# Halving the first sequence's opening: transposes, split and decay products by half the rows

## The reference

```python
h = rmsnorm(xn, pre_norm_w)
a = sigmoid(h @ w_a + decay_bias)           # decay
i = sigmoid(h @ w_i); v = h @ w_v
s = sqrt(clip(1 - a*a, 1e-8)) * (i * v)
rec = chunked_scan(a, s)                    # state = a * state + s
y = xn + rec @ out_proj_w
attn = y + (silu(gate) * up) @ w_down       # gate, up = rmsnorm(y) @ w_gate_up
moe = top-2 of 8 experts, each relu(xn @ w_fc)**2 @ w_proj, router logits xn @ w_router
```

## Time and profile before

| what | value |
|---|---|
| median of 3 runs | 288.89 us (288.81 to 288.93) |
| span of the profiled execution | 286.9 us |
| median less span | 1.99 us |
| PE busy | 279.4 us, 97% of the span |
| DVE, ACT, POOL busy | 202.7, 170.9, 145.8 us |
| granted PE clock | 9 tenths or more in all 40 slices |

### The profile page before, as it was taken

The page is one execution under the profiler, slowest core; times in us unless marked ns, Lnnn a source line. Parts: engine busy times, 40 slices in busy tenths (PEclk is TensorE's granted clock), DMA queues, the critical chain, the costliest instruction groups (busy, mean ns, idle before and its releaser), DMA issues.

```text
span 286.9 us, 5651 instructions
## 1 busy us (share of the span) xinstructions
PE 279.4 (97%) x1825; PEld 249.2 (87%) x1825; DVE 202.7 (71%) x467; ACT 170.9 (60%) x365; POOL 145.8 (51%) x138
## 2 busy tenths in 40 slices
PE   6999999999999999999999899999999999999995
PEld 5888988888988898898998789989989999888895
DVE  3899899989988978836558686555446545446973
ACT  3797967999759555536675545437477545432331
POOL 5498020433750135864877777666786776620000
PEclk9999999999999999999999999999999999999999
DMA  6999990017995011444244444344344534449922
GB/s 210 344 377 383 386 409 0 0 11 113 243 267 115 0 40 39 76 68 64 56 77 70 75 64 73 62 69 61 61 78 77 84 62 56 55 84 358 331 75 73
DMA packets 32584, 36.92 MB, mean 129 GB/s; under 512 B 4390, under 2 KB 29740, under 8 KB 32524
## 3 DMA queue, kind: packets, MB, share of 16 engines
q0 software_dynamic: 9616, 13.01, 28.2%
q1 hardware_dynamic: 20672, 21.31, 22.4%
q10 hardware_dynamic: 2268, 2.23, 2.2%
HBM read 24.68 MB, written 13.96 MB: 135 GB/s over the span
## 4 chain that ended last, share of the span: by engine, by line
PE 90%; DVE 5%; POOL 2%; issue 2%; ACT 1%; POOLq 0%; ACTq 0%; DVEq 0%
PE ps L396 75%; PE ps L656 6%; PE ps L479 5%; PE ps L400 1%; PE ps L492 1%; PE ps L413 1%; DVE hT_lo L1087 1%; POOL rn L1504 1%; DVE Wpj_lo L1247 1%; DVE stats L1059 0%; DVE X L1080 0%; DVE dec L1118 0%; POOL Waiv_raw L1541 0%; PE ps L507 0%; DVE xgT_lo L1322 0%
## 5 line engine op out<-in xcount | busy, mean ns | idle before, releaser
L1552 POOL DMA_INDIRECT xg<-xh_dram,gather_u x39 | 46.6, 1195 | 47.4 <-DVE picks L1314 34.8
L1561 POOL DMA_INDIRECT acc_dram<-yb,gather_u x39 | 61.9, 1587 | 16.3 <-issue 9.4
L396 PE MATMUL ps<-h2T_lo,Wgu_hi 128*128 128x512 f32 (+1 forms) x132 | 42.9, 386 | 0.0
L396 PE MATMUL ps<-h2T_hi,Wgu_hi 128*128 128x512 f32 (+1 forms) x132 | 40.9, 391 | 0.0
L396 PE MATMUL ps<-h2T_hi,Wgu_lo 128*128 128x512 f32 (+1 forms) x132 | 40.1, 385 | 0.0
L396 PE MATMUL ps<-Wd_hi,guT_hi 128*128 128x256 f32 x128 | 36.3, 284 | 0.1
L1331 DVE TENSOR_TENSOR aT_lo<-ps,aT_hi 128x256 fp32r<-128x256 f32 x39 | 16.6, 425 | 27.9 <-ACT aT_hi L911 21.1
L396 PE MATMUL ps<-Wd_hi,guT_lo 128*128 128x256 f32 x128 | 36.1, 282 | 0.0
L396 PE MATMUL ps<-Wd_lo,guT_hi 128*128 128x256 f32 x128 | 36.1, 282 | 0.0
L1252 DVE TENSOR_TENSOR gu<-gu,ps 128x512 f32<-128x512 f32 x31 | 21.2, 684 | 14.0 <-PE ps L396 10.9
L869 ACT ACTIVATE gu<-ps 128x512 f32<-128x512 f32 x31 | 18.4, 595 | 20.2 <-PE ps L396 20.2
(11 more groups left out here) (190 smaller groups left out, 683.7 us busy)
## 6 DMA issues: line engine op xcount, KB each, us to landing
sums<-acc_dram SPq DMA_DIRECT2D x8, 512.0 KB, 7.8
acc_dram<-zero SPq DMA_DIRECT2D x1, 2176.0 KB, 14.8
Wgu_raw<-in_L_attn_w_gate_up_dram SPq DMA_DIRECT2D x4, 512.0 KB, 9.3
Wfc_raw<-in_L_ffn_w_fc_dram SPq DMA_DIRECT2D x4, 512.0 KB, 13.7
xh_dram<-X ACTq DMA_DIRECT2D x4, 512.0 KB, 7.9
Wpj_raw<-in_L_ffn_w_proj_dram SPq DMA_DIRECT2D x4, 512.0 KB, 9.8
X<-in_L_attn_x_dram SPq DMA_DIRECT2D x3, 512.0 KB, 6.3
out_dram<-X SPq DMA_DIRECT2D x3, 512.0 KB, 4.8
```

What stands on the lines that cost most here:

```text
L396: return nc.tensor.matmul(dst, lhs, rhs, start=start, stop=stop, skip_group_check=group)
L1552: pool.indirect_dma_start(out=xg[i % XG][:, :], out_offset=None, in_=xh_dram, in_offset=bass.IndirectOffsetOnAxis(ap=gather_u[:, i:i + 1], ...
L1561: pool.indirect_dma_start(out=acc_dram[i % 2], in_=yb[i % YB][:, :], in_offset=None, compute_op=ALU.add, out_offset=bass.IndirectOffsetOnA ...
```

## The change

In the first sequence (b = 0) three steps go by halves `h` of its rows (row tiles 0 and 1, then 2 and 3), each half 256 rows wide. `transpose_first(h)` transposes a half into a pair of banks of its own (0 and 1, then 4 and 5). `split_first(h)` makes the high part of both feature blocks of that half in one ACT instruction, and the low part in one DVE instruction. `first_gates(h, part)` does the products of n = 0 and n = 1 for that half: part 0 those with the high activation (8 matmuls 256 wide), part 1 those with the low one (4 matmuls). DVE normalises row tiles 1, 2 and 3, ACT only tile 0. The 6 fillers stand behind the first half's transposes, the 12 in front of the products are gone. Semaphore counts are shifted to match.

```diff
--- before.py
+++ after.py
@@ -216,6 +216,7 @@
         var_ready, rstd_ready = sem("var_ready"), sem("rstd_ready")
         xh_ready, xh_half = [sem(f"xh_ready{b}") for b in range(B)], sem("xh_half")
         xh_stored = [sem(f"xh_stored{b}") for b in range(B)]
+        xT_half, hT_first_hi, hT_first_lo = sem("xT_half"), sem("hT_first_hi"), sem("hT_first_lo")
         xT_done, hT_hi, hT_split, wr_hi, wr_split = sem("xT_done"), sem("hT_hi"), sem("hT_split"), sem("wr_hi"), sem("wr_split")
         logit_done, logit_copied = sem("logit_done"), sem("logit_copied")
         tables_ready, q_ready = sem("tables_ready"), sem("q_ready")
@@ -400,24 +401,47 @@
                     nc.tensor.matmul(ps[:, bank, 0:P], ones_bf[:, :], before[:, :], start=True, stop=True)
 
             def transpose_x(c):
-                if c:
-                    pe.wait_ge(xh_ready[c], 1)
-                    pe.wait_ge(hT_split, K * c)
-
-                for j in (0, 1, 3, 2) if c == 0 else range(J):
-                    if (c, j) == (0, 3):
-                        keep_clock(6, 7)
-                    if c == 0:
-                        pe.wait_ge((xh_ready[0], xh_half)[j % 2], j // 2 + 1)
+                pe.wait_ge(xh_ready[c], 1)
+                if c > 1:
+                    pe.wait_ge(hT_split, K * (c - 1))
+
+                for j in range(J):
                     for k in range(K):
                         last = nc.tensor.transpose(ps[:, TX + k, j * P:(j + 1) * P], X[c][:, j, k * P:(k + 1) * P],
                                                    ident[:, :])
                 last.then_inc(xT_done, 1)
 
+            def transpose_first(h):
+
+                for j in (2 * h, 2 * h + 1):
+                    pe.wait_ge(*((xh_ready[0], 1) if j == 0 else (xh_half, j)))
+                    for k in range(K):
+                        last = nc.tensor.transpose(ps[:, TX + 4 * h + k, (j % 2) * P:(j % 2 + 1) * P],
+                                                   X[0][:, j, k * P:(k + 1) * P], ident[:, :])
+                last.then_inc(xT_half, 1)
+
+            def first_gates(h, part):
+
+                cols = slice(h * S // 2, (h + 1) * S // 2)
+                if part == 0:
+                    pe.wait_ge(hT_first_hi, h + 1)
+                else:
+                    pe.wait_ge(hT_first_lo, h + 1)
+                for l in (0, 1) if part == 0 else (0,):
+                    for k in range(K):
+                        if h == 0 and part == 0:
+                            pe.wait_ge(w_first_lo if l else w_half, k + 1)
+                        for n in range(2):
+                            last = product(ps[:, rec_bank(0, n), cols], Waiv[l][:, k, n * P:(n + 1) * P],
+                                           hT[0][part][:, k, cols], h + part + l + k == 0, part == 1 and k == K - 1, True)
+                            if h == part == 1 and k == K - 1:
+                                last.then_inc(aiv_done, 1)
+
             def logits(c):
 
-                pe.wait_ge(hT_split, K * (c + 1))
-                if c == 0:
+                if c:
+                    pe.wait_ge(hT_split, K * c)
+                else:
                     pe.wait_ge(wr_split, 1)
                 for j in range(J):
                     t = J * c + j
@@ -432,31 +456,19 @@
             def aiv(b, n):
 
                 what, r = n // 2, n % 2
-                if n == 0 and b:
-                    pe.wait_ge(hT_hi, K * (b + 1))
+                if n == 0:
+                    pe.wait_ge(hT_hi, K * b)
                 p = 6 * b + n - 5
                 if p >= 0:
                     pe.wait_ge(*rec_taken(p // 6, p % 6))
                 col = what * D + r * P
-                if (b, n) == (0, 0):
-
-                    pe.wait_ge(w_hi, 1)
-                    for k in range(K):
-                        pe.wait_ge(hT_hi, k + 1)
-                        for l in range(2):
-                            if l == 1:
-                                pe.wait_ge(w_first_lo, k + 1)
-                            product(ps[:, rec_bank(0, 0), :], Waiv[l][:, k, 0:P], hT[0][0][:, k, :], k + l == 0, False)
-                    for k in range(K):
-                        pe.wait_ge(hT_split, k + 1)
-                        last = product(ps[:, rec_bank(0, 0), :], Waiv[0][:, k, 0:P], hT[0][1][:, k, :], False, k == K - 1)
-                for m, (l, h) in enumerate((PRODUCTS if b == 0 else ((0, 0), (1, 0), (0, 1))) if b + n else ()):
+                for m, (l, h) in enumerate(PRODUCTS if b == 0 else ((0, 0), (1, 0), (0, 1))):
                     if b == 0 and m == 0 and r == 0:
-                        pe.wait_ge(w_hi, what + 1)
+                        pe.wait_ge(w_hi, what)
                     if b == 0 and l == 1 and r == 0:
                         pe.wait_ge(w_lo, what)
                     if n == 0 and m == 2:
-                        pe.wait_ge(hT_split, K * (b + 1))
+                        pe.wait_ge(hT_split, K * b)
                     for k in range(K):
                         last = product(ps[:, rec_bank(b, n), :], Waiv[l][:, k, col:col + P], hT[b][h][:, k, :],
                                        m + k == 0, m == 2 and k == K - 1)
@@ -468,7 +480,7 @@
                     pe.wait_ge(rec_ready, K * (b + 1))
                     if b == 0:
                         pe.wait_ge(wo_loaded, 16)
-                        pe.wait_ge(hT_split, K * B)
+                        pe.wait_ge(hT_split, K * (B - 1))
                     elif b == 1:
                         pe.wait_ge(routed, 1)
                         pe.wait_ge(count_taken, 1)
@@ -591,10 +603,13 @@
             pe.wait_ge(smalls_loaded, 48)
             nc.tensor.transpose(ps[:, 6, 0:3 * K], small_rows[:, :], ident[0:3 * K, 0:3 * K]).then_inc(smalls_turned, 1)
             keep_clock(8, 7)
-            transpose_x(0)
-            keep_clock(12, 7)
-            aiv(0, 0)
-            aiv(0, 1)
+            transpose_first(0)
+            keep_clock(6, 7)
+            first_gates(0, 0)
+            transpose_first(1)
+            first_gates(0, 1)
+            first_gates(1, 0)
+            first_gates(1, 1)
             aiv(0, 2)
             aiv(0, 3)
             logits(0)
@@ -763,7 +778,7 @@
                     act.wait_ge(w_loaded[0], 16)
                 hi, lo, raw = pieces[0][1]
                 A.activation(hi[:, k, :], raw[:, k, :], ACT.Copy,
-                             scale=smalls[:, PRE_W + k:PRE_W + k + 1]).then_inc(*((w_half, 1) if k == 0 else (w_hi, 1)))
+                             scale=smalls[:, PRE_W + k:PRE_W + k + 1]).then_inc(w_half, 1)
 
             def weights_hi(n):
                 if n == UNDER_SCAN:
@@ -787,6 +802,12 @@
                 A.activation(X[0][:, 2 * h, :], X[0][:, 2 * h, :], ACT.Identity, scale=rn1[:, 2 * h:2 * h + 1],
                              bias=nb1[:, 2 * h:2 * h + 1]).then_inc(xh_ready[0], 1)
 
+            def split_first(h):
+                act.wait_ge(xT_half, h + 1)
+                cols = slice(h * S // 2, (h + 1) * S // 2)
+                A.activation(hT[0][0][:, :, cols], ps[:, TX + 4 * h:TX + 4 * h + 2, 0:S // 2],
+                             ACT.Copy).then_inc(hT_first_hi, 1)
+
             def normalise_x(c):
                 act.wait_ge(rstd_ready, c + 2)
                 for j in range(J):
@@ -796,13 +817,13 @@
                 last.then_inc(xh_ready[c], 1)
 
             def store_xh(c):
-                act.wait_ge(xh_ready[c], 1 if c else 2)
+                act.wait_ge(xh_ready[c], 1)
                 if c == 0:
-                    act.wait_ge(xh_half, 2)
+                    act.wait_ge(xh_half, 3)
                 act.dma_start(xh_t[c], X[c][:, :, :]).then_inc(xh_stored[c], 16)
 
             def split_h(c):
-                act.wait_ge(xT_done, c + 1)
+                act.wait_ge(xT_done, c)
                 if c == 3:
                     act.wait_ge(aiv_done, 6)
                 for k in range(K):
@@ -926,9 +947,9 @@
             normalise_first(0)
             act.wait_ge(smalls_ready, 1)
             gates_hi_first(0)
-            normalise_first(1)
             gates_hi_first(1)
-            split_h(0)
+            split_first(0)
+            split_first(1)
             weights_hi(1)
             weights_hi(2)
             split_router()
@@ -1069,9 +1090,15 @@
             def normalise_first(h):
 
                 dve.wait_ge(rstd_ready, h + 1)
-                t = 2 * h + 1
-                V.tensor_scalar(X[0][:, t, :], X[0][:, t, :], mv[:, t, 0:1], rn1[:, t:t + 1],
-                                ALU.subtract, ALU.mult).then_inc(xh_half, 1)
+                for t in (1,) if h == 0 else (2, 3):
+                    V.tensor_scalar(X[0][:, t, :], X[0][:, t, :], mv[:, t, 0:1], rn1[:, t:t + 1],
+                                    ALU.subtract, ALU.mult).then_inc(xh_half, 1)
+
+            def split_first(h):
+                dve.wait_ge(hT_first_hi, h + 1)
+                cols = slice(h * S // 2, (h + 1) * S // 2)
```

(10 more changed lines are left out.)

## The result

| | before | after |
|---|---|---|
| median of 7 runs | 288.81 us (288.14 to 289.01) | 289.63 us (289.41 to 290.94) |
| ratio | | 1.0039, 95% interval 1.0025 to 1.0052 |
| span of the profiled execution | 286.9 us | 287.8 us |
| start of `transpose_x(2)` in the trace | 20.77 | 21.60 |

The change makes the kernel slower: by 0.82 us (0.3%) by the medians, by 1.1 us (0.39%, interval 0.7 to 1.5 us) by the ratio. The forecast was 289.8 in 289.3 to 290.3, slower with a chance of 0.75. In the traces `transpose_x(2)` starts 0.83 later and the span is 0.9 longer, so the loss is made before that point, and nothing behind it gives it back.

A forecast was written before the change was run, and what follows sets the result against it. The prediction took PE to bound the kernel (busy 97% of the span), with POOL's path meeting PE's at `transpose_x(2)`. POOL's root, 0.90 us late, carried through: 288.89 + 0.90 = 289.8 us, range 289.3 to 290.3.

The forecast's parts named there:

- The place in PE's queue: Second half's transposes queue behind eight first-half products on PE: 1.43 us later, making ACT's `weights_hi(1)` 0.95 late.
- PE's new wait: PE waits 0.86 us for POOL's low part of `w_i` before the third product of `aiv(0, 2)`, until 14.00.
- Two paths: POOL's and PE's paths meet at `transpose_x(2)`: POOL's, 0.90 us later at 21.67, covers PE's own at 21.35.
- The term that was a little large: PE's first transposes end at 7.74 as before, `split_first(0)` starts at 7.77; part of the +0.90 us.
- 256 columns: `first_gates` matmuls on PE take 0.12 us each, 0.08 more after a wait; halving costs 0.14 of PE.
- The clock: Rival: PE falls to half pace from 8.4 to the stall, adding 1.4 us: +2.3, 291.2; chance 0.08.
- Not slower: Rival: POOL's low part of `w_i` isn't late, no stall on PE: 288.8, no difference; chance 0.16.
- PE alone: Rival: POOL and DVE catch up 0.3 us, PE's 21.35 sets `transpose_x(2)`: +0.58, 289.47; chance 0.10.

The follow-up runs named there:

- e1: Changed kernel with the second half's transposes ahead of the first half's products on PE: 287.97 us against 288.47 before the change, ratio 0.9983.
- e7: Kernel before the change plus two idle copies on ACT between `split_h(0)` and `weights_hi(1)`: 289.05 us against 288.40, ratio 1.0025.
- e2: Changed kernel with `weights_hi(1)` between the two `split_first` on ACT: 288.66 us against 288.47 before the change, ratio 1.0006.
- e6: e1 with the products of n = 0 and 1 whole, 12 matmuls of 512 columns: 288.22 us against 288.40 before the change, ratio 0.9991.
- e4: Kernel before the change without its 12 fillers in front of the products: 288.35 us against 288.47, ratio 1.0003.
- e5: Changed kernel with the moves of e1 and e2 together: 287.70 us against 288.40 before the change, ratio 0.9966.
- e3: Changed kernel with row tile 2 normalised on ACT again: 289.61 us against 288.47 before the change, ratio 1.0042.
- e8: e5 with POOL doing the first operation of `gates_lo(2)` before `root_x(3)`: 287.62 us against 288.40 before the change, ratio 0.9972.

## Why the prediction was right

- **The place in PE's queue.** Forecast: the second half's transposes start at 9.44, `split_first(1)` on ACT at 10.08, `weights_hi(1)` at 10.57, POOL at 11.57. Measured: 9.34, 9.97, 10.47, 11.44. e1 takes this step away, and with it the whole loss.
- **PE's new wait.** Forecast 0.86 before the third product at 14.00, measured 0.62 in brackets, at 13.90. The listed idle time counts from the modelled end of the matmul before. From the pitch (two matmuls of 0.23 behind 12.64, so 13.10) to 13.90 it is 0.80.
- **Two paths.** Forecast: POOL's path (+0.90) covers PE's own (+0.75 by the third product). Measured: PE still waits 0.22 for DVE at 21.60, so POOL's path decided, at +0.83. The third product came 0.65 late. e7 showed that the late weights alone carry about all of the loss, e2 that with early weights DVE's late variances still cost 0.3 in the trace. One reading was too tight: PE was not 0.17 early before, as its listed wait says, but about 0.32. The last pair of products starts at 19.99, and where nothing is waited for (e6) the transposes follow a pair by 0.45. PE alone would have been ready at 20.76 + 0.45 = 21.21 and not at 21.35.
- **The term that was a little large.** The first transposes were taken to end at 7.74, as in the trace of before; in the changed kernel's they ended at 7.59. `split_first(0)` was thus 0.14 earlier than forecast, POOL's start 0.13. The root then began 0.11 behind POOL's low part (13.95 against 12.56 + 1.28), where 0.05 had been taken, and that leaves the 0.07 between 0.90 and 0.83. The pace of the first transposes belongs to the execution and not to the change (last section). Counted from DVE's normalisation for the second half, `transpose_x(2)` starts 14.21 us later in the changed kernel, 13.46 in the kernel before, and 13.27 in e4, whose early transposes were quick: 0.75 to 0.94 of loss. That the traces' 0.83 falls together with the 0.82 of the medians is partly luck.
- **256 columns.** The pitch is (8.86 - 8.29) / 4 = 0.14 for the first four and (9.34 - 8.86) / 4 = 0.12 for the next: 0.12 and a late first of 0.09, as taken from the earlier trace rows (0.12 and 0.08). The Trainium skill ("TensorE: Matmul & The Clock Gate", "Back-to-back issue gap") gives 262 cycles for 256 columns, an estimate of 0.109 us at full clock; these float32 products took 0.12, and the measurement decides.
- **The rivals.** The clock: PE's pitch was that of full pace behind every gap, and e4 has no loss with 0.78 idle. The Trainium skill ("TensorE: Matmul & The Clock Gate", "Why this matters for your kernels") advises against idle gaps between bursts of matmuls; it speaks of longer ones than the 0.2 to 0.8 us here, so it gives no ground for this rival, and no run here tests its advice. Not slower: it would have needed `weights_hi(1)` by 9.8; it came at 10.47, and in e1 at 9.10, which gave that outcome. PE alone: excluded by the 0.22 of waiting.

What was not forecast is how good the early order is. The prediction set a limit of 0.62 us of gain at PE's products if all its waits were gone (11.72 for the start of `aiv(0, 2)`); in e5 it starts at 11.56, since the second half's transposes fit into the time of ACT's first split, and POOL's root starts at 12.45 instead of 13.12. The measured gain of e5, 0.6 to 1.3 us, has that limit at its lower end.

## What to carry to other kernels

When work is cut into halves to start sooner, put the step that feeds the other engines (here the second half's transposes) ahead of the first half's own products: its input was ready 1.2 us before it ran. Look for the slack that isn't in the chain of waits, here the 0.23 us between POOL's last weight and PE's need of it; a delay larger than that becomes a wait on the busiest engine. And where an engine has idle time in front of a wait, see what stands behind the wait that could be done in it: `weights_hi(1)`, 0.90 us long, fitted into ACT's 1.74 us. Then ask of each halved step whether it gains anything once the order is right: the halved products were 0.56 us faster on PE, and `transpose_x(2)` started no earlier for it (e6).

## What the runs showed of the hardware

The first four transposes are the same instructions at the same place in every one of these kernels, yet their group lasts about 1.1 us in the earlier trace rows and in e2, e3, e5 and e8, and 0.66 in e4, e6 and e7. Here e6:

```profile
6.60 0.66 PE L419 MATMUL ps<-ident,X 128*128 128x128 f32 x4 [0.33 <-ACT X L795]
```

Here e5:

```profile
6.69 1.12 PE L419 MATMUL ps<-ident,X 128*128 128x128 f32 x4
```

The granted clock is given as 1.00, the 2.4 GHz level, from 3 us on in all ten profiles; only the pitch shows when PE reaches full pace. The small matmuls stand 0.107 us apart before and 0.055 after. In e6 and e7 they stand 0.055 apart from 5.7 on, in the kernel before from 7.8 on (not 7.5, as the prediction read it), in the changed kernel from 7.4 on, and in e8 the second half's transposes still take 0.21 each up to 8.7, where all kernels had issued the same small matmuls from 2.83 on. It moves the opening by up to 0.45 us. It may be a part of the spread of the runs of one kernel (288.14 to 289.01 before); that was not tried. Single traces of this kernel can be compared at one point of the opening to about that figure only, unless the comparison starts behind the transposes of the first sequence.
